# Weight loads from ACT's queue to SP's inside layer 0, context memsets on POOL, diagonal weights ahead of the first norm

## The reference

```
x += tanh(g_xattn[0]) * attention0(ctx, norm(x))   # 16 heads of 8, Wq/Wk/Wv 8x8 shared by the heads, masked softmax, Wo
x += tanh(g_ffn[0])   * experts(norm(x))           # top-1 of 8 experts plus a shared one, 128 -> 256 -> 128
x += tanh(g_xattn[1]) * attention1(ctx, norm(x))   # 16 heads of 64, with biases
x += tanh(g_ffn[1])   * bitlinear_ffn(norm(x))     # ternary weights, 8-bit activations, 128 -> 512 -> 128
```

## Time and profile before

| | us |
|---|---|
| median of 3 runs (lowest, highest) | 1271.19 (1270.29, 1271.75) |
| the profiled execution | 1269.61 |
| its span | 1267.3 |
| busy: PE, DVE, ACT, POOL | 1134.1 (89%), 888.6 (70%), 698.9 (55%), 509.4 (40%) |
| transfers, mean over the span | 119 GB/s |

### The profile page before, as it was taken

One profiled execution on the slowest core, in us unless ns is written; L12 is line 12 of the kernel. 1 busy time (PEld: TensorE's weight loads), 2 busy tenths in 40 slices (PEclk: granted clock), 3 DMA queues, 4 the chain that ended last, 5 costly groups with the idle time before them and its releaser, 6 DMA issues.

```text
span 1267.3 us, 27942 instructions
## 1 busy us (share of the span) xinstructions
PE 1134.1 (89%) x10056; PEld 649.4 (51%) x10056; DVE 888.6 (70%) x1250; ACT 698.9 (55%) x967; POOL 509.4 (40%) x344
## 2 busy tenths in 40 slices
PE   0669899999999999788797999999999999999984
PEld 0225555665656656633443555555555555555542
DVE  6466666666666675487777887767686877768668
ACT  0435455555555554545476666656666666666642
POOL 5148756667567641342303322323232323322220
PEclk9979899999999999789998999999999999999996
DMA  5145455455544552200005776766577666767630
GB/s 158 53 145 170 121 177 159 149 162 172 162 151 154 159 157 54 63 1 26 1 1 94 147 150 139 143 128 147 117 146 142 135 142 129 143 137 148 115 66 15
DMA packets 222262, 151.29 MB, mean 119 GB/s; under 512 B 184576, under 2 KB 195312, under 8 KB 222208
## 3 DMA queue, kind: packets, MB, share of 16 engines
q1 hardware_dynamic: 215952, 147.40, 48.5%
q10 hardware_dynamic: 6256, 3.16, 1.0%
HBM read 62.23 MB, written 25.39 MB: 69 GB/s over the span
## 4 chain that ended last, share of the span: by engine, by line
PE 75%; DVE 9%; issue 6%; ACT 6%; ACTq 3%; DMA 0%; POOL 0%; DVEq 0%; POOLq 0%; SPq 0%
PE bank L848 17%; PE bank L866 16%; PE bank L723 7%; PE bank L816 6%; PE bank L747 6%; PE bank L751 5%; PE bank L764 4%; ACTq L386 3%; DVE region L1692 2%; PE bank L824 2%; ACT region L1196 2%; DVE e_row L1503 2%; PE bank L888 2%; PE bank L794 2%; PE bank L1089 2%
## 5 line engine op out<-in xcount | busy, mean ns | idle before, releaser
L1503 DVE CUSTOM_DVE_ANT_0 e_row<-bank,region 112x1500 f32<-112x1500 f32 x128 | 220.1, 1720 | 125.1 <-PE bank L723 123.7
L1196 ACT ACTIVATE region<-bank 125x896 f32<-125x896 f32 x192 | 176.0, 917 | 201.3 <-PE bank L751 201.3
L1542 DVE TENSOR_REDUCE neg_max<-bank 128x1 f32<-128x1500 f32 x112 | 192.7, 1720 | 130.1 <-PE bank L848 130.1
L848 PE MATMUL bank<-region 128*128 128x500 f16 x1008 | 235.1, 379 | 3.2 <-ACT e_row L1223 1.8
L1232 ACT COPY region<-bank 128x768 f16<-128x768 f16 x224 | 177.8, 794 | 89.0 <-PE bank L816 89.0
L1223 ACT ACTIVATE e_row<-bank,neg_shift 128x1500 f32<-128x1500 f32 x112 | 169.2, 1510 | 68.2 <-DVE neg_shift L1546 38.6
L549 POOL CAST u_w<-e_row 128x1500 f16<-128x1500 f32 x56 | 80.6, 1440 | 216.1 <-ACT e_row L1223 216.1
L549 POOL CAST wg_sb<-e_row 128x1500 f16<-128x1500 f32 x56 | 81.8, 1461 | 197.7 <-ACT e_row L1223 153.6
L848 PEld LDWEIGHTS bank<-region 128*128 (+1 forms) x1008 | 97.2, 98 | 108.0 <-issue 3.5
L747 PE MATMUL bank<-row_of,region 112*128 112x448 bf16 x384 | 137.7, 359 | 7.7 <-ACT region L1196 7.7
L751 PE MATMUL bank<-region 97*128 (+1 forms) x768 | 137.6, 260 | 0.0
(11 more groups left out here) (218 smaller groups left out, 1519.7 us busy)
## 6 DMA issues: line engine op xcount, KB each, us to landing
region<-region SPq DMA_DIRECT2D x192, 96.0 KB, 2.2
turned_rows<-region SPq DMA_DIRECT2D x16, 768.0 KB, 3.8
region<-turned_rows SPq DMA_DIRECT2D x32, 384.0 KB, 3.5
c_in<-in_ctx SPq DMA_DIRECT2D x16, 750.0 KB
split_rows<-region SPq DMA_DIRECT2D x16, 750.0 KB
region<-in_mask_Bx1xSxS_if SPq DMA_DIRECT2D x32, 328.1 KB
region<-split_rows SPq DMA_DIRECT2D x24, 250.0 KB
g_w<-split_rows SPq DMA_DIRECT2D x24, 250.0 KB
```

The source lines that it names most:

```text
L848: last = pe.matmul(score_banks1(par, t)[:, k, :], q1[:, ql, b, 128 * t:128 * (t + 1)], c_t1[par][:, cl, 4 * k:4 * k + 4, 0:KP], start=(ql ...
L1196: act.activation(p0[:, 2 * i:2 * i + 2, :], ring0("s", h, i)[0:KP, :, 0:HALF_ROWS], ACT.Exp, scale=SCALE0)\
L1503: dve.tensor_tensor_reduce(out=masked.rearrange("p (a k) -> p a k", a=3), in0=bank[0:R0, 0:3, 0:4 * KP], in1=mask_bias[par][:].rearrange(" ...
L1542: dve.tensor_reduce(neg_max[:, t:t + 1], score_banks1(par, t), AX.XY, ALU.max, negate=True)\
```

## The change

- ACT keeps only the two gate loads. SP issues gate_w and g_w at the end of its part of batch 0, u_w in batch 1, and the small and ternary weights in batch 14.
- POOL scales g_w in batch 14 and u_w in batch 15.
- POOL clears c_pv and c_sum, behind the pads and ahead of the first split.
- DVE forms the diagonal weights ahead of the seven norms, and PE multiplies them ahead of the transposes.

```
@@ sync, layer0 @@
                     if not (isinstance(b, int) and b + 2 >= B):
                         sync_load_mask(sp, b + 2)
+                    if first:
+                        load(sp, "in_ffn0", [(gate_w_sb[:], gate_w)])
+                        load_ffn0(g_w, rt_gate, sh_gate)
+                    elif isinstance(b, int) and b == 1:
+                        load_ffn0(u_w, rt_up, sh_up)
+                    elif isinstance(b, int):
+                        load_small()
+            def load_ffn0(w, routed, shared):
+                load(sp, "in_ffn0", [(w[:, 0:NE, :], routed.rearrange("e h i -> h e i")), (w[:, NE, :], shared)])
+            def load_small():
...
+                sp.wait_ge(sem("const_0"), 11)
+                load(sp, "in_w1", [(bq1_pad[0:64, :, 0], bq[0]), (bq1_pad[64:128, :, 1], bq[1]),
+                                   (bo1_col[:], bo1.rearrange("(e o) -> e o", o=1))])
+                for two in range(2):
+                    load(sp, "in_bv", [(bv1_col[64 * two:64 * two + 64], bkv[two, 1])])
...
@@ gpsimd @@
             pool.wait_ge(sem("pad0"), 3)
+            for p in range(2):
+                pool.memset(c_pv[p][:], 0.0).then_inc(sem("pv_zero"), 1)
+                pool.memset(c_sum[p][:], 0.0).then_inc(sem("pv_zero"), 1)
+            pool.wait_ge(sem("pv_zero"), 4)
+            for p in range(2):
+                pool.memset(c_pv[p][:, :, :, 0:1], 1.0).then_inc(sem("pv_const"), 1)
+                pool.memset(c_sum[p][:, :, 0:1], float(KC)).then_inc(sem("pv_const"), 1)
@@ gpsimd, layer0 @@
-                if isinstance(b, int) and b < 2:
+                if isinstance(b, int) and b >= B - 2:
                     pool.wait_ge(sem("in_ffn0"), 16 * 5)
-                    w = (g_w, u_w)[b]
+                    w = (g_w, u_w)[b - (B - 2)]
@@ tensor @@
-            pe_norm_t(pe, 0)
             pe.wait_ge(sem("diag"), 3)
             pe.matmul(bank[:, 2, 0:E], block_diag[:, 0, :], block_diag[:, 1, :], start=True, stop=True)\
                 .then_inc(sem("w0_made"), 1)
+            pe_norm_t(pe, 0)
@@ scalar @@
-            load(act, "in_ffn0", [
...
-            act.wait_ge(sem("const_0"), 1)
...
-            load(act, "in_w1", [(bq1_pad[0:64, :, 0], bq[0]), (bq1_pad[64:128, :, 1], bq[1]),
...
-                load(act, "in_bv", [(bv1_col[64 * two:64 * two + 64], bkv[two, 1])])
-            load(act, "in_wf", [(wg_sb[:, 0], w_gate.rearrange("(j p) h -> p j h", p=128)),
...
@@ vector @@
-            dve_norm(dve, 0, range(TT))
             dve.wait_ge(sem("in_w8"), 16 * 3)
             dve.wait_ge(sem("const"), 10)
             for n in range(3):
 ...
+            dve_norm(dve, 0, range(TT))
...
-            for p in range(2):
-                dve.memset(c_pv[p][:], 0.0).then_inc(sem("pv_zero"), 1)
-                dve.memset(c_sum[p][:], 0.0).then_inc(sem("pv_zero"), 1)
...
```

More of the change, by code:

```diff
@@ L492, in layer0 @@
                         sync_load_mask(sp, b + 2)
+                    if first:
[8 more added lines that the diff above has]
+            def load_small():
+                bq = bq1.rearrange("(k two p) -> two p k", two=2, p=D1)
+                bkv = bkv1.rearrange("(k two part d) -> two part d k", two=2, part=2, d=D1)
+                sp.wait_ge(sem("const_0"), 11)
[3 more added lines that the diff above has]
+                    load(sp, "in_bv", [(bv1_col[64 * two:64 * two + 64], bkv[two, 1])])
+                load(sp, "in_wf", [(wg_sb[:, 0], w_gate.rearrange("(j p) h -> p j h", p=128)),
+                                   (wg_sb[:, 1], w_up.rearrange("(j p) h -> p j h", p=128)),
+                                   (wg_sb[:, 2], w_down.rearrange("h (j p) -> h j p", p=128))])
             sync_split_out(sp, 0)
@@ L1260, in _ @@
                                    (gates[:, 2:4], g_ffn.rearrange("(o n) -> o n", o=1).broadcast_to((128, 2)))])
-            load(act, "in_ffn0", [
[L1262 to L1265, removed]
-            act.wait_ge(sem("const_0"), 1)
-            bq = bq1.rearrange("(k two p) -> two p k", two=2, p=D1)
-            load(act, "in_w1", [(bq1_pad[0:64, :, 0], bq[0]), (bq1_pad[64:128, :, 1], bq[1]),
-                                (bo1_col[:], bo1.rearrange("(e o) -> e o", o=1))])
-            for two in range(2):
-                load(act, "in_bv", [(bv1_col[64 * two:64 * two + 64], bkv[two, 1])])
-            load(act, "in_wf", [(wg_sb[:, 0], w_gate.rearrange("(j p) h -> p j h", p=128)),
-                                (wg_sb[:, 1], w_up.rearrange("(j p) h -> p j h", p=128)),
-                                (wg_sb[:, 2], w_down.rearrange("h (j p) -> h j p", p=128))])
             act.wait_ge(sem("in_gates"), 32)
```

## The result

| us | before | changed |
|---|---|---|
| median of 4 runs (lowest, highest) | 1270.74 (1270.29, 1271.75) | 1247.21 (1245.02, 1248.69) |
| the profiled execution, its span | 1269.61, 1267.3 | 1247.09, 1245.3 |

The ratio is 0.9814, 95% interval 0.9802 to 0.9825: 23.5 us faster, where 11 had been forecast. The time lies within the range given; the direction was right, the size half of what came.

The account below looks back on a forecast made before the run. The prediction took ACT's sequencer issuing transfers to bound the opening, from 0.8 to 39.8 us. Its sum was 1269.6 - 10.1 (opening) + 0 + 0.2 (scaling of u_w) = 1259.7, given as 1259.5 us, range 1246 to 1264.

Parts of the forecast that it names:

- Part 1: Opening: loads leave ACT, whose transfer issues held it; with nothing else changed, the first query product starts 23.8 us sooner.
- Part 2: Opening, memsets on POOL: norms end at 21.3, copies wait for the mask, q0_low starts at 33.5; opening gains 10.1 us.
- Exactly one: Opening: between two POOL instructions exactly one DVE norm gets through; norms end at about 21.3 instead of 15.6.
- (a): Opening: the v_heads copies don't wait for POOL, only the norms do; gain 18.2, time 1251.4; chance 0.25.
- the restart of PE: Opening: PE restarts slowly after its stall, costing 0 to 3 us; 1 taken.
- (b): Opening: norms keep ahead of POOL's memsets as a burst, q0_low starts near 21.6; gain 23, time 1246.6; chance 0.12.
- (c): Opening: POOL's f32 memsets go by bytes, making everything 5.3 us later; time 1264.8; chance 0.08.
- (d): Opening as forecast, but batch 14's scaling misses L1514 or PE's stall is absorbed: 6 less, 1253.7; chance 0.07.
- (e): Batch 14: small loads hold SP 99 us, PE waits for layer 1's weights; time 1329; chance 0.04.
- (f): Opening: nothing gained, since another wait stands there; chance 0.01.
- Part 3: POOL's scaling moves from batches 0, 1 to 14, 15: minus 6 us, plus 6; net 0, bounds -7 and +2.
- Part 4: Loads on SP in batches 0, 1 and 14: covered by PE's work and by slack, cost 0.

Follow-up runs that it names:

- the back-to-back kernel: The changed kernel with POOL's four memsets in the order c_pv, c_pv, c_sum, c_sum instead of c_pv, c_sum, c_pv, c_sum: 1248.88 us.
- c_split0 first: The changed kernel with only POOL's clearing of c_split0 moved ahead of its rstd instructions: 1256.54 us.
- the combined version: The changed kernel with c_split0 ahead of rstd, c_pv/c_sum memsets waiting behind the copies, g_w scaled in batch 14's gap, expert weights loaded in the opening: 1237.16 us.

## Why the prediction was right or wrong

**What bounds the opening, Part 1: right.** ACT's copies stand directly behind the transposes (19.50 in the chain), and DVE's norms are what PE waits for. The diagonal weights didn't delay the first norm. The bound of 23.8 held: the opening gave 22.2. But the loads by themselves gave only 7.4, since the v_heads copies then meet POOL's subtraction and mask; the rest needs the other two edits.

**Part 2: the failed step** is the one that has the v_heads copies "come at about 23.7", into POOL's split, wait for the mask, and put the first q0_low at 33.5. (The text says "in its cast"; by its own ends, 23.3 and 26.4, they would have come in the subtraction, which changes nothing in the sum.) They came at 19.84 and waited for the end of one memset. Nearly all of the 3.9 us between is when the norms ended, 17.66 and not 21.3, and that is the count of norms per POOL instruction: "norms 1 and 2 by 14.6, then c_pv, one norm, c_sum, one norm, c_pv". Norms in the timeline of the changed kernel, the fourth row being the fifth and sixth together:

```profile
11.35 2.67 DVE L1503 TENSOR_SCALAR x_norm<-x_tok,mean_var,rstd 128x128 f32<-128x128 f32 x1 [1.21 <-POOL rstd L568]
...
14.00 0.33 DVE L1503 TENSOR_SCALAR x_norm<-x_tok,mean_var,rstd 128x128 f32<-128x128 f32 x1
14.25 0.34 DVE L1503 TENSOR_SCALAR x_norm<-x_tok,mean_var,rstd 128x128 f32<-128x128 f32 x1
14.51 2.82 DVE L1503 TENSOR_SCALAR x_norm<-x_tok,mean_var,rstd 128x128 f32<-128x128 f32 x2
...
17.25 0.41 DVE L1503 TENSOR_SCALAR x_norm<-x_tok,mean_var,rstd 128x128 f32<-128x128 f32 x1
```

Four were through by 14.6, the fifth (2.75 by itself) and the sixth stood behind the first c_pv (to 17.33), the seventh passed beside the short c_sum, and none met the second c_pv. So they ended 3.6 sooner, and the copies came before the cast at 21.01.

Two counts were wrong. Four norms, not two, were ahead of the first c_pv. And behind a long memset two norms come through and not one, 0.07 apart: so behind c_pv here (14.51 and 2.82 in the fourth row), between the two memsets in the back-to-back kernel, and in the kernels with c_split0 first or the diagonal weights late; one more passes beside c_sum. "Exactly one" was read from the earlier trace rows, where POOL's instruction is a tensor_tensor, which reads SBUF, and there it holds; it doesn't carry over to a memset. Why the two differ no run tests. Both counts were needed: with only two ahead, the norms end at 20.19 (the late diagonal weights); with four ahead and one per POOL instruction, the seventh would still stand behind the second c_pv, as it does in the back-to-back kernel (20.06).

The same step has a third fault: it queues the a_heads products behind the last norm, 2.4 of the 23.7. It cost nothing in the changed kernel, since no norm was waiting when they came, but the back-to-back memsets show that they don't stand in that line; there the norms ended at 20.06, near the forecast's order, and the copies still came before the cast. With this alone put right, the forecast's own copies come at some 21.4, while POOL is at its last memsets (to 21.8). I knew that this meeting decided between 10 and 18 us (rival (a) says it), and took the late arrival as given.

The sizes in that step were sound: the memsets took 2.73 and 0.43 (2.7, 0.3), the turns are real, and copies that do meet the split and mask took 8.02, 7.25 and 9.44 in three kernels, where they take 0.43 by themselves. Only the restart of PE was wrong for the changed kernel: I charged 1 us, and from the first q0_low to the batch-0 mark it took 66.26, before 66.25. Nor had the stage begun cold before, as I wrote: from 42 to 60 us PE's granted clock was 1.00. In the kernel with the diagonal weights late, where PE did stall, it took 68.82, and the granted clock from 30 to 42 us was 0.86.

The two norms that got ahead are no chance of one run. In the three kernels with the diagonal weights behind the norms (the one before among them) the first norm took 3.00 us and waited for POOL's short memsets too; in the five with them ahead and c_split0 behind rstd it took 2.67 and was through at the end of c_split0, so that two more norms passed before 14.6 beside the short memsets. Why the order of earlier work shifts that turn was not settled.

The lock itself is in the traces: a norm of 0.33 us took 2.75 beside a memset of 2.73 and ended with it, as the Trainium skill (SBUF — State Buffer, "Who interferes with whom") has it. The same section of the Trainium skill exempts an instruction with at most one SBUF input outside the 2-port modes, and the traces agree: the a_heads products took 1.88 beside a memset and without one. The forecast named this rule and didn't apply it to them.

**Rivals.** (a), gain 18.2 because copies don't wait: refuted, they do. (b), 1246.6 with copies that meet only memsets and a first q0_low near 21.6: its time (1247.2) and its consequence (22.44) came, its reason, the burst, is refuted by the back-to-back memsets. The measured time is near that of (b) for another reason than (b)'s, and that it lies in the stated range is owed to (b)'s being in it. (c), memsets by bytes: refuted by 2.73. (d): refuted by 4.73 in batch 14. (e), SP held 99 us: refuted, the eight loads took 6.5 us. (f): refuted.

**Part 3: right.** Minus 7.1 in batch 1, plus 7.0 in batch 14, where I had said 6 for both; the scaling of u_w was covered. The experiment that moves it confirms the place and the price, 7.3 by the marks and 7.5 in the medians.

**Part 4: nearly right.** Priced at 0. The small loads were covered. The big ones made POOL wait twice for its context, some 1.3 to 1.8 us by the marks, too little to show in the medians.

**The sum.** Measured -22.2 in the opening, -0.2 for the scaling, +1.5 for the loads, -1.1 behind the last mark: -22.0, the difference of the spans. The forecast has 12.1 too little for the opening, and no other term is off by more than 1.5.

## What to carry to other kernels

Where two engines share a lock, price a short instruction by when it arrives in the other engine's queue, not by its own length: 0.43 us of copies took 0.52 or 9.44, by whether they came ahead of the other engine's cast. Work put on the other engine can then be a shield, as the memsets here, and moving some out of the way can cost (2.65 us moved ahead, 9.3 lost). The sure way is to order the two by a semaphore: in the combined version, whose semaphore holds the memsets back, norms and copies took 1.88 and 0.42. What the semaphore alone is worth in time was not measured. A count of turns read at one kind of instruction (tensor_tensor) need not hold at another (memset). When such a step decides between two outcomes, compute the arrival with each instruction's own rule for waiting, and if the margin is under the error of the sum, forecast both.

## What was not expected of the hardware

- A memset on POOL, which reads nothing, holds a DVE tensor_scalar or copy from SBUF to SBUF until it ends: norms of 0.33 took 2.75 beside c_pv's 2.73, and when it ends two of them come through, where one does behind a tensor_tensor.
- DVE goes on past a waiting instruction: in the back-to-back kernel the a_heads products are recorded from 18.10 while the norm of 17.31 waited until 20.06, and all ended with it. One kernel's trace shows it.
- The same issue of a transfer with single numbers as rows took 19.72 us on ACT, behind the 2.4 MB of g_w and u_w in its queue, and 0.63 on SP in batch 14, without them. Whether it was the bytes ahead or something else that held it, no run separates.
